# Last layer of a four-layer transformer chain on one core: conditioned weights and first chunks laid among the attention's heads, SiLU one block ahead of rounding, ffn stages in another order

## The reference, cut to what matters

```python
x = x + _L3_attn_ref(...)                      # 16 causal heads of width 8, softmax
out  = einsum('btc,oc->bto', x, W_base) + b_base
lora = einsum('bter,eor,be->bto', einsum('btc,erc->bter', x, As), Bs, w)
y = out + lora * 2.0                           # _L3_cond2_ref
h = silu(tlin(y, w1)) * tlin(y, w2)            # 128 -> 512
h = gelu(tlin(h, h1))                          # 512 -> 512
h = gelu(tlin(h, h2))                          # 512 -> 512
x = x + tlin(h, w3)                            # 512 -> 128, all of _L3_ffn_ref
```

## Time and profile before

| | us |
|---|---|
| median of 3 runs | 1317.19 (1313.71 to 1318.36) |
| the profiled execution | 1312.5 |
| its span | 1310.6 |
| PE busy | 1209.5 (92%) |
| DVE busy | 824.5 (63%) |
| ACT busy | 647.9 (49%) |
| POOL busy | 275.4 (21%) |

### The profile page before, as it was taken

One profiled execution on the slowest core, in us unless ns is written; L12 is line 12 of the kernel. 1 busy time (PEld: TensorE's weight loads), 2 busy tenths in 40 slices (PEclk: granted clock), 3 DMA queues, 4 the chain that ended last, 5 costly groups with the idle time before them and its releaser, 6 DMA issues.

```text
span 1310.6 us, 28370 instructions
## 1 busy us (share of the span) xinstructions
PE 1209.5 (92%) x10425; PEld 970.9 (74%) x10425; DVE 824.5 (63%) x1740; ACT 647.9 (49%) x1327; POOL 275.4 (21%) x356
## 2 busy tenths in 40 slices
PE   8899867889999899999999999899999999988999
PEld 5667423568888799877788887499889876656777
DVE  7988697654565667566776465566564477754342
ACT  4678584354334244444444444244434367655553
POOL 7677001200023134220000023134230032100000
PEclk9999988999999999999999999999999999999999
DMA  9000202310503132105034002032111000000000
GB/s 327 11 2 2 81 1 94 123 65 1 217 13 109 48 102 66 33 16 217 1 145 182 1 15 62 10 114 71 36 55 48 1 3 3 3 2 1 1 17 17
DMA packets 43332, 75.87 MB, mean 58 GB/s; under 512 B 3896, under 2 KB 34240, under 8 KB 42304
## 3 DMA queue, kind: packets, MB, share of 16 engines
q1 hardware_dynamic: 39104, 65.66, 13.8%
q0 software_dynamic: 4096, 8.40, 2.2%
HBM read 59.75 MB, written 14.29 MB: 56 GB/s over the span
## 4 chain that ended last, share of the span: by engine, by line
PE 73%; DVE 16%; ACT 6%; issue 3%; DVEq 1%; DMA 0%; POOL 0%; ACTq 0%; POOLq 0%
PE banks L1987 8%; PE banks L1998 7%; PE banks L1983 7%; PE banks L2042 5%; PE banks L1974 4%; PE banks L2052 3%; PE banks L1712 3%; PE banks L1717 3%; PE banks L1719 3%; PE banks L1718 3%; PE banks L1967 2%; PE banks L1969 2%; PE banks L1968 2%; DVE SC L2336 2%; PE banks L1850 2%
## 5 line engine op out<-in xcount | busy, mean ns | idle before, releaser
L2249 ACT ACTIVATE SC<-banks 128x512 f32<-128x512 f32 x192 | 114.4, 596 | 224.4 <-PE banks L1983 126.8
L2336 DVE SCALAR_TENSOR_TENSOR SC<-banks,SM,SC 128x512 f32<-128x512 f32 x128 | 95.8, 748 | 121.9 <-PE banks L1987 103.3
L1998 PE MATMUL banks<-A,SC 128*128 x1024 | 137.1, 277 | 7.8 <-DVE SC L2336 7.1
L1987 PE MATMUL banks<-X,SC 128*128 128x128 f32 x1024 | 136.9, 277 | 4.2 <-DVE SC L2609 3.6
L1983 PEld LDWEIGHTS banks<-X,SC 128*128 128x128 f32 x1024 | 126.1, 192 | 19.5 <-issue 12.5
L1983 PE MATMUL banks<-X,SC 128*128 128x128 f32 x1024 | 136.1, 276 | 4.4 <-ACT SC L2233 3.2
L1998 PEld LDWEIGHTS banks<-A,SC 128*128 128x128 f32 x1024 | 125.3, 192 | 17.4 <-issue 16.5
L1987 PEld LDWEIGHTS banks<-X,SC 128*128 128x128 f32 x1024 | 124.5, 192 | 6.7 <-DVE SC L2609 6.4
L2042 PE MATMUL banks<-A 128*128 128x128 f32 x736 | 100.4, 280 | 11.8 <-DVE A L2759 6.2
L2042 PEld LDWEIGHTS banks<-A 128*128 128x128 f32 x736 | 90.1, 193 | 16.6 <-ACT A L2274 9.2
L2233 ACT ACTIVATE SC<-A 128x512 f32 x128 | 80.6, 630 | 28.3 <-PE banks L1987 22.9
(11 more groups left out here) (348 smaller groups left out, 2528.3 us busy)
## 6 DMA issues: line engine op xcount, KB each, us to landing
A<-in_moe SPq DMA_DIRECT2D x36, 768.0 KB, 10.0
A<-xs SPq DMA_DIRECT2D x20, 256.0 KB, 3.5
ys<-A SPq DMA_DIRECT2D x20, 256.0 KB, 2.4
BW<-in_l1f SPq DMA_DIRECT2D x2, 2048.0 KB, 7.4
BW<-in_l2f SPq DMA_DIRECT2D x1, 3456.0 KB, 11.8
BW<-in_l1c SPq DMA_DIRECT2D x1, 3072.0 KB, 16.2
BW<-in_l3f SPq DMA_DIRECT2D x1, 2816.0 KB, 9.6
A<-in_l1c SPq DMA_DIRECT2D x1, 2560.0 KB, 8.5
```

The lines of the kernel that those rows point to most:

```text
L1987: m = e.matmul(at["pu"].ap[:, cut(q)], wx[:, cut(4 + q)], x, start=True, stop=True)
L1998: m = e.matmul(o, at["h"].ap[:, cut(q)], W[:, bass.ds(r + (1024 + 128 * q), 128)], start=k == 0 and q == 0, stop=k == 1 and q == 3)
L2249: e.activation(at["h"].ap, at["pg"].ap, ACT.Gelu_apprx_tanh).then_inc(at["gelu"][0], 1)
L2336: return e.scalar_tensor_tensor(out=o, in0=a, scalar=s, in1=b, op0=o1, op1=o2)
```

## The change

1. `cond_items` splits `all3`: for layer 3 an item {scale; product and add} that needs nothing, and an item {cx} that needs `("x3", n)`.
2. Seven items are put among the heads: after head 12 {scale, cw, add} of chunk 0, after head 15 cx of chunk 0, after head 17 `l3_y` of chunk 0, after head 20 {scale, cw, add} of chunk 1, after head 23 cx 1, after head 25 `l3_y` 1, after head 28 {scale, cw, add} of chunk 2. Each takes a round of its own.
3. After head 31: an empty item, {scale, cw, add} of chunk 3, `silu_next`, an empty item, cx 2, up0, cx 3, and the rest of the new `turns`.
4. `silu_next` is a one-column SiLU on ACT into a scratch column.
5. `l3_y` no longer waits for `("x3", 3)`, but for the end of the earlier sparse layer; `l3_up`'s roundings and remainders wait for `("x3", 3)` instead.
6. In `l3_up` ACT issues silu 0, silu 1, round 0, silu 2, round 1, silu 3, round 2, round 3; DVE issues product 0, product 1, remainder 0, product 2, and so on. Before, each was finished for block m before block m+1.
7. The stages after up1: hidden-a 0, hidden-a 1, y2, y3, hidden-b 0, hidden-b 1, out0, up2, out1, up3, hidden-a 2, hidden-a 3 and on as before.

The diff, without the parts that only rewrite `l3_up` on DVE in the same manner as on ACT:

```diff
                 if src_key:
-                    items.append(([(src_key, n)], [all3, s1], (key, n)))
+                    items.append((([], [scale, lambda product=product, add=add: (product(), add())], None), ([(src_key, n)], [s1], (key, n))))
...
-                    at = step("l3_y", n=n, ready=sig["y3b", n], over=sig["x3", 3], y=RY3.take())
+                    at = step("l3_y", n=n, ready=sig["y3b", n], over=sig["moe4_over"], y=RY3.take())
...
-            turns = [(n, 0) for n in (0, 1)] + [(n, k) for k in (1, 2) for n in (0, 1)]
-            turns += [(2, 0), (0, 3), (1, 3), (2, 1), (0, 4), (1, 4), (3, 0), (3, 1), (2, 2), (3, 2), (2, 3), (3, 3),
-                      (2, 4), (3, 4)]
-            return [([("y3b", n)], [stages[n][k]], None) for n, k in turns]
+            return [[([("y3b", n)], [f], None) for f in stages[n]] for n in range(NC)]
...
-        seq = (items + flat(seq[12:]) + flat(mix(m3, f2, m4, shared_items())) + at3 + cond_items("y3b", 3, "x3")
-               + l3_ffn_items())
+        cond3, ffn3 = cond_items("y3b", 3, "x3"), l3_ffn_items()
+
+        def silu_next():
+            step("silu_next", to=sm(1))
+
+        heads3 = [k for k, it in enumerate(at3) if len(it[1]) > 3]
+        assert len(heads3) == 32
+        beside3 = {12: cond3[0][0], 15: cond3[0][1], 17: ffn3[0][0], 20: cond3[1][0], 23: cond3[1][1], 25: ffn3[1][0],
+                   28: cond3[2][0]}
+        end3 = []
+        for k, it in enumerate(at3):
+            end3.append(it)
+            if k in heads3 and heads3.index(k) in beside3:
+                end3.append(beside3[heads3.index(k)])
+        nothing = ([], [lambda: None], None)
+        end3 += [nothing, cond3[3][0], ([], [silu_next], None), nothing, cond3[2][1]]
+        turns = [(0, 1), None, (1, 1), (0, 2), (1, 2), (2, 0), (3, 0), (0, 3), (1, 3), (0, 4), (2, 1), (1, 4), (3, 1),
+                 (2, 2), (3, 2), (2, 3), (3, 3), (2, 4), (3, 4)]
+        end3 += [ffn3[t[0]][t[1]] if t else cond3[3][1] for t in turns]
+        seq = items + flat(seq[12:]) + flat(mix(m3, f2, m4, shared_items())) + end3
...
+                elif kind == "silu_next":
+                    e.activation(at["to"], c("s1")[:, 0:1], ACT.Silu)
...
-                    for m in range(4):
-                        over(at["r"][m])
-                        w.wait_ge(*at["mm"][2 * m])
-                        e.activation(at["r"][m].ap, at["pg"][m].ap, ACT.Silu,
-                                     scale=c("s1")[:, m:m + 1]).then_inc(at["silu"][m][0], 1)
-                        w.wait_ge(*at["mul"][m])
-                        e.activation(at["h"].ap[:, 512 * m:512 * m + 512], at["r"][m].ap, ACT.Copy).then_inc(at["hi"][m][0], 1)
+                    for m in range(5):
+                        if m < 4:
+                            over(at["r"][m])
+                            w.wait_ge(*at["mm"][2 * m])
+                            e.activation(at["r"][m].ap, at["pg"][m].ap, ACT.Silu, scale=c("s1")[:, m:m + 1]).then_inc(at["silu"][m][0], 1)
+                        if m > 0:
+                            k = m - 1
+                            w.wait_ge(*at["after"])
+                            w.wait_ge(*at["mul"][k])
+                            e.activation(at["h"].ap[:, 512 * k:512 * k + 512], at["r"][k].ap, ACT.Copy).then_inc(at["hi"][k][0], 1)
```

More of the change, by code:

```diff
@@ L306, in add @@
                     ring.give(at["pa"], at["sum"])
[L308 to L311, removed]
                 def s1(n=n, st=st, ring=ring):
@@ L1565, in s0 @@
                     h = RH3.take()
-                    at = step("l3_up", y=u["y"], h=h, ready=[sig["l3w"]] + u["ty"], pg=[], pu=[], r=[], mm=[], silu=[],
+                    at = step("l3_up", y=u["y"], h=h, after=sig["x3", 3], ready=[sig["l3w"]] + u["ty"], pg=[], pu=[], r=[], mm=[], silu=[],
                               mul=[], hi=[], lo=[])
-                    for m in range(4):
[L1569 to L1581, removed]
+                    for m in range(5):
+                        if m < 4:
+                            pg, pu = RA.take(), RA.take()
+                            at["pg"].append(pg)
+                            at["pu"].append(pu)
+                            at["r"].append(RS4.take())
+                            at["mm"] += [tick("l3_mm"), tick("l3_mm")]
+                            at["silu"].append(tick("l3_act"))
+                            RA.give(pg, at["silu"][m])
+                            at["mul"].append(tick("l3_vec"))
+                            RA.give(pu, at["mul"][m])
+                        if m > 0:
+                            at["hi"].append(tick("l3_act"))
+                            at["lo"].append(tick("l3_vec"))
+                            RS4.give(at["r"][m - 1], at["hi"][m - 1], at["lo"][m - 1])
+                            u[m - 1] = [at["hi"][m - 1], at["lo"][m - 1]]
                     RY3.give(u["y"], at["mm"][7])
@@ L2865, in _ @@
                     over(at["h"])
[L2866 to L2873, removed]
+                    for m in range(5):
+                        if m < 4:
+                            r = at["r"][m].ap
+                            w.wait_ge(*at["silu"][m])
+                            w.wait_ge(*at["mm"][2 * m + 1])
+                            stt(r, at["pu"][m].ap, c("s2")[:, m:m + 1], r, ALU.mult, ALU.mult).then_inc(at["mul"][m][0], 1)
+                        if m > 0:
+                            k = m - 1
+                            w.wait_ge(*at["after"])
+                            w.wait_ge(*at["hi"][k])
+                            e.tensor_tensor(at["h"].ap[:, 2048 + 512 * k:2560 + 512 * k], at["r"][k].ap,
+                                            at["h"].ap[:, 512 * k:512 * k + 512], ALU.subtract).then_inc(at["lo"][k][0], 1)
                 elif kind == "l3_hid":
```

## The result

The changed kernel took 1323.29 us in the median of 8 runs (1320.46 to 1325.9), the kernel before 1317.24 in 8 runs of the same session (1312.68 to 1318.71). The ratio is 1.0047, 95% interval 1.0034 to 1.006: slower by 6 us. That is just inside the 0.5% that the prediction called no change, but the interval doesn't reach 1, so it is a small slowdown and not nothing. The forecast of 1319.5 was 3.8 us too low.

What follows compares the result with a forecast made beforehand. PE was taken as the bound, so only its idle time could be won. A gain of 9.7 us and a loss of 12.0 gave +2.3 on the median 1317.2, so 1319.5 us, range 1307 to 1328.

Steps and rivals of the forecast that it cites:

- B: Feed-forward part, up0 to the last matmul: 10.5 us of excess, of which the change gains 9.7.
- A: Head 12's scores to up0: PE idles 19.5 us against 7.5 before, a loss of 12.0.
- The walk: Queues followed through heads 12 to 31 with prices from the trace; 19.5 us of PE idle time.
- all four cases: The prediction's own case, chance 0.50, and three rivals, chances 0.24, 0.16 and 0.10.
- rival 2: Among the heads: PE's clock falls in long stalls, two to four falls, 5.6 to 11.2 us, 1325 to 1331; chance 0.16.
- Its kinds: Stalls among the heads: addition 5.9 us, y's remainder 4.8, projections 1.8, smaller 3.7, last rounds 2.1, chunk 3 1.2.
- The lower bound: Among the heads: seven holes at 0.5 us and other items make 8.6 idle, a loss of 1.
- The price in the rival: One clock fall, taken from a 2.81 us PE stall in an earlier layer: 2.8 us lost.
- The first: Among the heads: items are taken in, holes cost 0.5 us each, loss about 1 to 2, time 1309; chance 0.24.
- The third: Feed-forward part: banks, not ACT's order, hold PE; gain 4 us instead of 9.7, time 1325; chance 0.10.
- the prediction's own sign: Granted clock under 0.95 in the windows of the heads would mean that the clock falls.
- The rule on interleaving: Heads and feed-forward: interleaving may help stretches with different busiest engines; by it the sum would be near the 18 us ceiling.

Runs made afterwards that it cites:

- holes_only: The kernel before with seven empty items at the places of the inserted ones, no instruction added; 1319.58 us, ratio 1.0058.
- filled: The changed kernel with eight unused matmuls on PE ahead of the four long waits among the heads; 1312.39 us, ratio 1.001.
- tail_only: The changed kernel with nothing among the heads, all conditioning behind head 31, new feed-forward order kept; 1300.04 us, ratio 0.9911.
- hung_rc: The changed kernel, items hung on existing heads' stages without own rounds, addition behind the maxima, y's remainder one head later, banks from RC; 1304.51 us, ratio 0.9914.
- y_as_holes: The changed kernel with the rounds of y0 and y1 left empty and both rounded after head 31; 1319.85 us, ratio 1.0034.
- heads_only: The changed kernel's items among the heads, with the old feed-forward part and no silu_next; 1327.55 us, ratio 1.0117.
- changed_again: The changed kernel measured once more without any edit, in a later session; 1319.97 us, ratio 1.0027 to the kernel before.
- add_third: The changed kernel with the conditioning's addition one round later, behind the softmax, and its banks from RC; 1314.55 us, ratio 0.9979.

## Why the prediction was right, and where it was not

It forecast no change that can be told, with a small plus. The plus came, 1323.29 against 1319.5 forecast and inside 1307 to 1328, and the mechanism of both stretches was the one named. But -9.7 in B and +12.0 in A had given +2.3; measured are -7.5 and +13.5, with the cx that moved from A to B taken out of both (1.05 us) -8.6 and +14.5, so +5.9.

Part of its being right is luck. The walk had 2.3 us too much idle time in A, which hid half of the clock's 4.85; those stood in no term of the sum. The range was wide enough to hold all four cases, that of the clock with up to three falls, so the number alone says little: 1323.29 lies nearer to the 1325 at which rival 2 begins than to 1319.5. And 0.5% was too coarse for what can be told: the interval of the ratio is 0.13% to each side.

- **Stretch A, idle time.** The walk gave 19.5 us idle, the trace 17.2. Its kinds held nearly one by one: scores 15 forecast 2.8, measured 2.83; scores 23, 2.3 and 2.23; transposes 17, 2.6 and 2.30; transposes 25, 2.2 and 1.70; the two waits for the addition 0.4 and 0.35; scores 19 and 27 behind the projections 0.9 and 0.78. Writing out the queues round by round was worth it. The lower bound was not: it took 0.5 for a hole from the earlier trace rows, and holes_only gives 1.06, so a loss of 1 was never near.
- **Stretch A, the clock.** This is the step that failed. The forecast put nothing in the sum for the clock and made it a rival with a chance of 0.16, for the reason that PE at 80% busy had kept its clock. The longest wait behind that row is 1.7 us, so it said nothing of one over 2; the earlier trace rows did. The clock fell at the stalls of 2.83, 2.30 and 2.23 us and stayed at 1.00 after 1.70. The price in the rival was that of a longer fall: 2.8 us for one that lasted 6.8, where those of the changed kernel lasted 3.4 and cost 1.6 each. It was read a little off, too: between the stall of 2.81 us and the twelve matmuls stand two more and another 0.85 us of waiting. With 4.85 for three falls added, the walk would have given +7.2. The Trainium skill (TensorE: Matmul & The Clock Gate, What's actually happening) has the array gated down when it idles; filled shows it here, since filling the idle time took the loss away.
- **Stretch B.** Forecast a gain of 9.7, measured 8.6. The step that was off is that up2 "now follows out0 (12 matmuls, 2.7 us), which covers the second table load". Time enough was there, but the load is issued behind the wait of the SiLU that needs it, so PE's work ahead of it covers nothing. It cost 0.96 us of PE and, by the runs with a second fetch, 1.15 to 1.33, which is the whole difference. SiLU ahead alone brought 2.3.
- **silu_next, the new waits on the addition, the outputs**: forecast at nothing, and in B there is no PE wait but the one at 1255.51.
- **The median.** The forecast added 4.7 us to the profiled time, since the profile lay that far below the median. The last section shows where in the kernel such a difference can arise.
- **Rivals.** The first (heads take the items in, 1309) falls with holes_only. The second happened: three falls at the stalls that the walk had found, and by the prediction's own sign, a clock under 0.95 in windows of the heads, it is the case that came. Only its size kept the time below 1325: 4.85 us instead of 8.4 for three. The third fell: no block waited for the gate's product but the one behind the second table load.
- **The rule on interleaving** (the Trainium skill, Perfetto Trace Analysis, Optimization Strategy). tail_only against the changed kernel shows that here laying the work among the heads in rounds of its own costs some 17 us (A and B together, 219.5 against 202.3), and hung_rc that without holes it gains next to nothing (202.1).

## What to carry to other kernels

Work that is put into a software pipeline of in-order queues costs what is queued behind its waits, and each round without an item of the pipeline costs a stall of its own, here 1 us; if it must go in, hang it on existing stages, with the instruction that waits behind the one that others need, and first add up how much idle time is left at its old place, here 2 us. Where a forecast holds TensorE stalls of the size seen here (2.2 to 2.8 us), put the clock into the sum, and take stalls of a changed kernel by a walk through the queues, not by the average busy share. The table load was hidden here only where an activation of that function stood ahead of the wait.

## What the runs showed of the hardware that was not expected

- Three falls of the clock cost 4.85 us together, and eight matmuls without use, put into the waits, won 4.6 back.
- The same stall does not always bring the same fall: in y_as_holes scores 23 waited 2.23 us too, and the clock in the 10 us behind it was 1.00; behind the 2.83 at scores 15 it was 0.75 over 6 us. In heads_only the clock was down for 6.8 us at scores 15, from inside the stall on, in the changed kernel for 3.4 us, from 1.1 us behind its end. What else decides it is open; it was not tried.
- Head 12 started between 1093.0 and 1103.6 us in these profiles, while A and B repeated within 0.12. A good part of that arises in one place, in an earlier, sparse layer. The same two DVE instructions, of before and of after:

```profile
842.52 0.43 DVE L2759 COPY A<-BW 128x512 f32 x1 [0.33 <-issue]
...
943.16 0.75 DVE L2336 SCALAR_TENSOR_TENSOR SC<-banks,SM,SC 128x512 f32<-128x512 f32 x1 [1.49 <-PE banks L1987]
```

```profile
840.79 0.43 DVE L2776 COPY A<-BW 128x512 f32 x1 [0.32 <-issue]
...
945.31 0.75 DVE L2353 SCALAR_TENSOR_TENSOR SC<-banks,SM,SC 128x512 f32<-128x512 f32 x1 [1.49 <-PE banks L1999]
```

They lie 100.6 us apart in before and 104.5 in after. In all thirteen profiles the distance is either 100.3 to 101.0 us (eight of them) or 103.9 to 104.7 (after, and the four of one session: changed_again, y_as_holes, add_third, hung_rc), with the clock of after at 1.00 from 842 to 909 us. Of the three later sessions this one also has the highest median of before, and in the session of the result the eight times of before fall into two groups, 1312.68 to 1313.71 (three) and 1317.19 to 1318.71 (five). So nearly 4 us can lie between two profiles, or perhaps two sessions, that the change has no part in. What sets it, and where the rest of the spread comes from, stays open.
